# Attention scores from a relu, two linear columns per head and one VectorE operation per tile, with a fourth tile of receivers' rows expanded from windows

## The reference

```python
x_l = (x @ W_l + b_l).reshape(n, H, F)
x_r = (x @ W_r + b_r).reshape(n, H, F)
e_emb = (ea @ W_e).reshape(-1, H, F)
m = jax.nn.leaky_relu(x_l[src] + x_r[dst] + e_emb, 0.2)
alpha = jnp.einsum('ehf,hf->eh', m, att)
```

## Time and profile before

| | us |
|---|---|
| median of 3 runs | 6645.43 |
| lowest and highest | 6640.19, 6647.89 |
| span of the profiled execution | 5191.8 |
| TensorE busy in the span | 4139.6 (80%) |
| VectorE busy | 3632.4 (70%) |
| ScalarE busy | 2012.0 (39%) |
| GpSimd busy | 2560.2 (49%) |

### The profile page before, as it was taken

The page is one execution under the profiler, slowest core; times in us unless marked ns, Lnnn a source line. Parts: engine busy times, 40 slices in busy tenths (PEclk is TensorE's granted clock), DMA queues, the critical chain, the costliest instruction groups (busy, mean ns, idle before and its releaser), DMA issues. The chain is left out here.

```text
span 5191.8 us, 87147 instructions
## 1 busy us (share of the span) xinstructions
PE 4139.6 (80%) x27186; PEld 3591.2 (69%) x27186; DVE 3632.4 (70%) x9778; ACT 2012.0 (39%) x4938; POOL 2560.2 (49%) x2806
## 2 busy tenths in 40 slices
PE   5710677758888999999489999998788778887888
PEld 5610566757786666666377777788788778877888
DVE  8977578857776888888789999977344434444554
ACT  6835344434443333333244444456122212221222
POOL 0010777667774666666100000014777577757775
PEclk9955778778888999999789999975888888888888
DMA  8023677757774444444122222235566556655665
GB/s 216 7 40 78 154 186 187 181 122 156 160 158 107 105 105 105 104 104 104 31 63 53 53 54 52 51 90 141 124 135 136 116 123 136 135 120 120 135 135 114
DMA packets 1642255, 583.18 MB, mean 112 GB/s; under 512 B 1548519, under 2 KB 1574950, under 8 KB 1641578
## 3 DMA queue, kind: packets, MB, share of 16 engines
q1 hardware_dynamic: 921158, 297.65, 25.3%
q10 hardware_dynamic: 636612, 195.74, 16.2%
q0 software_dynamic: 84064, 84.64, 8.8%
HBM read 381.77 MB, written 209.21 MB: 114 GB/s over the span
## 5 line engine op out<-in xcount | busy, mean ns | idle before, releaser
L2002 POOL DMA_INDIRECT early<-node_g,src_w x1173 | 1114.6, 950 | 426.2 <-issue 356.5
L2219 POOL DMA_INDIRECT early<-node_g,src_w x782 | 759.4, 971 | 296.7 <-issue 248.8
L2784 POOL TENSOR_TENSOR fbt_c<-x_sb,fbln 128x128 f32<-128x128 f32 x56 | 22.3, 399 | 1026.2 <-DVE fbln L2860 1026.2
L1115 POOL DMA_INDIRECT fscat<-node_g,early x392 | 370.6, 946 | 287.7 <-PE bank L1147 136.6
L1221 ACT ACTIVATE fsy<-bank 128x512 f32<-128x512 f32 x448 | 243.8, 544 | 439.3 <-DVE fslz L1264 155.7
L2263 PE MATMUL bank<-l0S,l0msg 128*128 128x128 f32 x1568 | 277.8, 358 | 152.3 <-DVE l0S L2361 62.3
L2263 PEld LDWEIGHTS bank<-l0S,l0msg 128*128 128x128 f32 x1568 | 267.8, 270 | 159.5 <-issue 92.4
L2554 PE MATMUL bank<-early,faS 128*128 128x256 f32 x1568 | 357.8, 386 | 0.0
L1264 DVE TENSOR_TENSOR fslz<-bank,fsy 128x512 f32<-128x512 f32 x448 | 267.0, 621 | 117.6 <-ACT fsy L1221 105.7
L2554 PEld LDWEIGHTS bank<-early,faS 128*128 128x128 f32 x1568 | 296.5, 192 | 73.8 <-issue 34.9
L2044 PE MATMUL bank<-l3S,l3msg 128*128 128x128 f32 x1568 | 230.9, 316 | 104.0 <-issue 64.5
(11 more groups left out here) (363 smaller groups left out, 10924.8 us busy)
## 6 DMA issues: line engine op xcount, KB each, us to landing
edge_h<-early SPq DMA_DIRECT2D x280, 224.0 KB
node_g<-amax ACTq DMA_DIRECT2D x224, 224.0 KB
early<-edge_h SPq DMA_DIRECT2D x168, 256.0 KB
early<-node_g,src_w POOLq DMA_INDIRECT x1955
l0msg<-edge_a ACTq DMA_DIRECT2D x56, 256.0 KB
l0msg<-edge_h SPq DMA_DIRECT2D x56, 256.0 KB
l1msg<-edge_h SPq DMA_DIRECT2D x56, 256.0 KB
alpha<-edge_h SPq DMA_DIRECT2D x56, 256.0 KB
```

The source lines that it names most:

```text
L1115: pool.indirect_dma_start(out=cat[:, s, t, 0:F], out_offset=None, in_=node_g, in_offset=bass.IndirectOffsetOnAxis(ap=src_i[:, col], axis=0 ...
L2002: pool.indirect_dma_start(out=ring[:, n % RING, t, :], out_offset=None, in_=table_in, in_offset=bass.IndirectOffsetOnAxis(ap=src_w[:, n * ...
L2219: pool.indirect_dma_start(out=ring[:, n % RING, t, :], out_offset=None, in_=table_in, in_offset=bass.IndirectOffsetOnAxis(ap=src_w[:, n * ...
```

## The change

The leaky relu is written as 0.8 relu(z) + 0.2 z. The part 0.2 z times `att`, summed over a head, is linear in the inputs, so it becomes a column of the weights: each head gets two more columns, the sum of weight times `att` and its negative (`FX = 66`, `HX = 264`). relu of the one minus relu of the other gives the linear part back, with factors 0.2 and -0.2 in `att_x`. One operation of VectorE for each tile, max with 0 and then times `att_x`, makes what ScalarE's scaling, the max and the multiplication made; the sum over a head runs over 66 columns. A tile has a bank to itself, counted by `z_ok` and `z_read`.

The bias product uses 128 rows, of which all but three are zero, and two tiles' bias products stand together. `EXPAND` goes from 3 to 4. `turn_edges` makes all transposes first and then the products with `spread`. The node numbers that are compared are made once, for all steps, instead of in each. `own_rows(n)` moves between `turn_edges(n)` and `turn_own(n + 1)`. The widened weights are made at the start of the stage, and the bias rows in `attention_weights` get the two columns as well. Indents are cut in the diff, and the counts on which SP and ScalarE wait, which only change their names, are left out.

```diff
-EXPAND = 3
+EXPAND = 4
...
+FX = F + 2
+HX = HEADS * FX
...
-b3_row = sb("b3_row", [3, HF], bf16)
+b3_row = sb("b3_row", [P, HX], bf16)
...
-lz = tb("lz", [P, 2, HS, HF]); ones3 = tb("ones3", [3, P], bf16)
-y = tb("y", [P, 2, 2, HF])
+lz = tb("lz", [P, 2, HS, HX]); ones_b = tb("ones_b", [P, P], bf16)
+Wlr_x = tb("Wlr_x", [2 * F, HX]); Wea_x = tb("Wea_x", [F + 1, HX]); Wself_x = tb("Wself_x", [2 * F, HX])
+att_x = tb("att_x", [P, HX]); first_i = tb("first_i", [1, T], i32)
+by_head = lambda ap: ap.rearrange("p (h f) -> p h f", h=HEADS)
+weights = [(Wlr_x, Wlr, 2 * F), (Wea_x, Wea, F + 1), (Wself_x, Wself, 2 * F)]
...
-ids_ps = bank[3][:, HF:HF + EXPAND * SPAN].rearrange("p (w t) -> p t w", w=SPAN)
+assert NS * EXPAND * SPAN <= 512
+ids_ps = bank[3][:, 0:NS * EXPAND * SPAN].rearrange("p (w n t) -> p n t w", w=SPAN, n=NS)
...
-block_no = lambda n, kind, k: (2 * n + kind) * NB + k
-z_bank = lambda g: bank[4 + g % 4]
-att_ps = bank[3][:, 0:HF].unsqueeze(1).to_broadcast((P, HS, HF))
+tile_no = lambda n, kind, t: (2 * n + kind) * HS + t
+z_bank = lambda g: bank[4 + g % 4][:, 0:HX]
...
         if n >= 1:
             pe.wait_ge(catT_ok, n)
+        if n == 0:
+            pe.wait_ge(spread_ok, 1)
+        place = [(b, t, slice((t - t0) * P, (t - t0 + 1) * P)) for b, (t0, t1) in enumerate(CH) for t in range(t0, t1)]
+        for b, t, col in place[EXPAND:]:
+            nc.tensor.transpose(bank[b][:, col], cat[:, s, t, :], ident[:, :])
+        for b, t, col in place[:EXPAND]:
+            nc.tensor.transpose(bank[b][0:F, col], cat[:, s, t, 0:F], ident[:, :])
         pe.wait_ge(near_in[s], 16 * EXPAND * (n // 2 + 1))
         pe.wait_ge(spread_ok, n + 1)
-        for b, (t0, t1) in enumerate(CH):
-            for t in range(t0, t1):
-                col = slice((t - t0) * P, (t - t0 + 1) * P)
-                if t < EXPAND:
-                    nc.tensor.transpose(bank[b][0:F, col], cat[:, s, t, 0:F], ident[:, :])
-                    for w in range(SPAN):
-                        ins = nc.tensor.matmul(bank[b][F:2 * F, col], near[:, s, t, w, :], spread[:, t, w, :], start=(w == 0), stop=(w == SPAN - 1))
-                else:
-                    ins = nc.tensor.transpose(bank[b][:, col], cat[:, s, t, :], ident[:, :])
+        for b, t, col in place[:EXPAND]:
+            for w in range(SPAN):
+                ins = nc.tensor.matmul(bank[b][F:2 * F, col], near[:, s, t, w, :], spread[:, t, w, :], start=(w == 0), stop=(w == SPAN - 1))
         ins.then_inc(cat_turned, 1)
...
-        for k, (t0, t1) in enumerate(PAIRS):
-            g = block_no(n, OWN, k)
-            if g >= 4:
-                pe.wait_ge(lz_ok, g - 3)
+        for t0, t1 in PAIRS:
             for t in range(t0, t1):
-                to = z_bank(g)[:, (t - t0) * HF:(t - t0 + 1) * HF]
-                nc.tensor.matmul(to, ones3[:, :], b3_row[:, :], start=True, stop=False)
-                ins = nc.tensor.matmul(to, selfT[:, s, t * P:(t + 1) * P], Wself[:, :], start=False, stop=True)
-            ins.then_inc(z_ok, 1)
+                g = tile_no(n, OWN, t)
+                if g >= 4:
+                    pe.wait_ge(z_read, g - 3)
+                nc.tensor.matmul(z_bank(g), ones_b[:, :], b3_row[:, :], start=True, stop=False)
+            for t in range(t0, t1):
+                to = z_bank(tile_no(n, OWN, t))
+                nc.tensor.matmul(to, selfT[:, s, t * P:(t + 1) * P], Wself_x[:, :], start=False, stop=True).then_inc(z_ok, 1)
...
-        for k, (t0, t1) in enumerate(PAIRS):
-            g = block_no(n, EDGE, k)
-            pe.wait_ge(lz_ok, g - 3)
-            for t in range(t0, t1):
-                to = z_bank(g)[:, (t - t0) * HF:(t - t0 + 1) * HF]
-                nc.tensor.matmul(to, catT[:, t * P:(t + 1) * P], Wlr[:, :], start=True, stop=False)
-                ins = nc.tensor.matmul(to, eaT[:, s, t * P:(t + 1) * P], Wea[0:F + 1, :], start=False, stop=True)
-            ins.then_inc(z_ok, 1)
-
-    pe.wait_ge(padded, 1)
+        for t in range(HS):
+            g = tile_no(n, EDGE, t)
+            pe.wait_ge(z_read, g - 3)
+            nc.tensor.matmul(z_bank(g), catT[:, t * P:(t + 1) * P], Wlr_x[:, :], start=True, stop=False)
+            nc.tensor.matmul(z_bank(g), eaT[:, s, t * P:(t + 1) * P], Wea_x[:, :], start=False, stop=True).then_inc(z_ok, 1)
...
+    pe.wait_ge(first_ok, 1)
...
+    pe.wait_ge(padded, 1)
+    pe.wait_ge(w_copied, 1)
     turn_own(0)
     own_rows(0)
     for n in range(NS):
         turn_edges(n)
+        if n >= 1:
+            own_rows(n)
         if n + 1 < NS:
             turn_own(n + 1)
         edge_tiles(n)
-        if n + 1 < NS:
-            own_rows(n + 1)
...
-    def leaky(n, kind):
-        for k, (t0, t1) in enumerate(PAIRS):
-            g = block_no(n, kind, k)
-            act.wait_ge(z_ok, g + 1)
-            if g >= 2:
-                act.wait_ge(lz_ok, g - 1)
-            A.activation(y[:, g % 2, 0:t1 - t0, :], z_bank(g)[:, 0:(t1 - t0) * HF].rearrange("p (t c) -> p t c", c=HF), ACT.Copy, scale=SLOPE).then_inc(y_ok, 1)
-
+    for to, w, n_rows in weights:
+        ins = A.copy(by_head(to[:, :])[:, :, 0:F], by_head(w[0:n_rows, :]))
+    ins.then_inc(w_copied, 1)
     turned_own(0)
-    leaky(0, OWN)
     for n in range(NS):
         turned_edges(n)
         if n + 1 < NS:
             turned_own(n + 1)
-        leaky(n, EDGE)
-        if n + 1 < NS:
-            leaky(n + 1, OWN)
...
-    v.memset(ones3[:, :], 1.0)
+    v.tensor_scalar(first_f[:, :], dst_f[0:1, :], float(NP - SPAN * P), None, ALU.min)
+    v.tensor_scalar(first_i[:, :], dst_f[0:1, :], float(NP - SPAN * P), None, ALU.min)
+    v.drain()
...
+    v.memset(ones_b[:, :], 1.0)
...
+    v.tensor_scalar(by_head(att_x[:, :])[:, :, 0:F], by_head(attb[:, :]), 1.0 - SLOPE, None, ALU.mult)
+    v.memset(by_head(att_x[:, :])[:, :, F:F + 1], SLOPE)
+    v.memset(by_head(att_x[:, :])[:, :, F + 1:FX], -SLOPE)
+    product = [lz[:, 0, k, 0:HF] for k in range(len(weights))]
+    for to, (_, w, n_rows) in zip(product, weights):
+        v.tensor_tensor(to[0:n_rows, :], w[0:n_rows, :], attb[0:n_rows, :], ALU.mult)
+    v.drain()
+    for of, (to, _, n_rows) in zip(product, weights):
+        v.tensor_reduce(by_head(to[:, :])[:, :, F], by_head(of[0:n_rows, :]), AX.X, ALU.add)
+    v.drain()
+    for to, _, _ in weights:
+        v.tensor_scalar(by_head(to[:, :])[:, :, F + 1], by_head(to[:, :])[:, :, F], -1.0, None, ALU.mult)
...
+    by_step = first_id[:, 0:NS * HS].rearrange("p (n t) -> p n t", t=HS)[:, :, 0:EXPAND]
+    for w in range(SPAN):
+        v.tensor_scalar(ids_ps[:, :, :, w], by_step, float(w * P), None, ALU.add)
+    v.drain()
...
     def expand(n):
-        own = first_id[:, n * HS:n * HS + EXPAND]
-        for w in range(SPAN):
-            v.tensor_scalar(ids_ps[:, :, w], own, float(w * P), None, ALU.add)
         dve.wait_ge(dst_in[n % 2], 16 * (n // 2 + 1))
         if n >= 1:
             dve.wait_ge(cat_turned, n)
-        v.drain()
         v.tensor_tensor(spread[:, :, :, :], dst_b[:, n % 2, :].rearrange("p (t e) -> p t e", t=EXPAND).unsqueeze(2).to_broadcast((P, EXPAND, SPAN, P)),
-                        ids_ps.unsqueeze(3).to_broadcast((P, EXPAND, SPAN, P)), ALU.is_equal).then_inc(spread_ok, 1)
-        v.drain()
-
-    def leaky(n, kind):
-        for k, (t0, t1) in enumerate(PAIRS):
-            g = block_no(n, kind, k)
-            dve.wait_ge(y_ok, g + 1)
-            v.tensor_tensor(lz[:, kind, t0:t1, :], z_bank(g)[:, 0:(t1 - t0) * HF].rearrange("p (t c) -> p t c", c=HF), y[:, g % 2, 0:t1 - t0, :], ALU.max).then_inc(lz_ok, 1)
-        v.drain()
-
+                        ids_ps[:, n, :, :].unsqueeze(3).to_broadcast((P, EXPAND, SPAN, P)), ALU.is_equal).then_inc(spread_ok, 1)
 
     def scores(n, kind):
-        leaky(n, kind)
+        for t in range(HS):
+            g = tile_no(n, kind, t)
+            dve.wait_ge(z_ok, g + 1)
+            v.scalar_tensor_tensor(lz[:, kind, t, :], z_bank(g), 0.0, att_x[:, :], ALU.max, ALU.mult).then_inc(z_read, 1)
+        v.drain()
         to = (amax, alpha)[kind][:, n * HS:(n + 1) * HS, :]
-        v.tensor_tensor(lz[:, kind, :, :], lz[:, kind, :, :], att_ps, ALU.mult)
-        v.drain()
-        v.tensor_reduce(to, lz[:, kind, :, :].rearrange("p t (h f) -> p t h f", h=HEADS), AX.X, ALU.add).then_inc(scored, 1)
+        v.tensor_reduce(to, lz[:, kind, :, :].rearrange("p t (h f) -> p t h f", h=HEADS), AX.X, ALU.add)
 
     expand(0)
-    scores(0, OWN)
     for n in range(NS):
+        scores(n, OWN)
         if n + 1 < NS:
             expand(n + 1)
         scores(n, EDGE)
-        if n + 1 < NS:
-            scores(n + 1, OWN)
+    v.drain()
...
+    v.memset(b3_row[:, :], 0.0)
...
-    left = brb[0:3, :]
+    v.tensor_copy(brx[:, :, 0:F], brb[0:3, :].rearrange("p (h f) -> p h f", h=HEADS))
+    v.tensor_tensor(b_lin[0:3, :], brb[0:3, :], attb[0:3, :], ALU.mult)
+    v.drain()
+    v.tensor_reduce(brx[:, :, F], b_lin[0:3, :].rearrange("p (h f) -> p h f", h=HEADS), AX.X, ALU.add)
+    v.drain()
```

(56 more changed lines are left out.)

2 lines of the change are left out of this document (removed).

## The result

The kernel after took 6600.5 us (median of 7 runs, 6572.24 to 6628.33) against 6646.74 for the kernel before (7 runs): ratio 0.9924, 95% interval 0.9899 to 0.9949. The forecast was 6554, range 6507 to 6612.

The account below looks back on a forecast made before the run. TensorE was taken to bound `edge_rows`: 2.9 + 4.4 + 0.6 + 6.26 + 0.4 = 14.6 us a step against 16.17, 88 us, plus 4 once; span 5100 plus 1453.6 gives 6554 us, range 6507 to 6612.

Parts of the forecast that it names:

- TensorE bounds the stage, and the step shrinks by the pieces named: In `edge_rows`, TensorE sets the step, which goes from 16.17 to 14.6 us, 88 us over 56 steps.
- edge tiles with their wait: In `edge_tiles`, 14 products of 264 columns take 6.26 us, plus 0.4 waiting for VectorE.
- the switch cost of `own_rows`: TensorE going over to the bias product and back: 0.1 us per group, 0.4 for four groups.
- the wait for the copy: Before the edge products, TensorE's 0.62 us idle for ScalarE's copy to `catT` goes, covered by `own_rows` products.
- a wait in mid-edge: TensorE waits 0.4 us for VectorE before the fifth edge tile of each step.
- The price from the 448-wide row: VectorE's fused operation at 264 columns, priced from a 0.620 us operation on 448 elements: 0.43 us.
- Rival 2: VectorE becomes the bound: fused operation 0.69 us, step 15.4, gain 47 us, time 6598; chance 0.08.
- Rival 1: In `own_rows`, data type causes the switch: 0.3 us per group, step 15.4, time 6598; chance 0.18.
- Rival 3: TensorE's granted clock falls in `edge_rows`: at 0.86 the step is 16.9 us, time 6680; chance 0.07.
- Program size hardly changes, so I hold the time outside the span still: Whole launch: the median's 1453.6 us above the span stays, added to a span of 5100 us.
- The 92 us of gain: Whole kernel: 88 us from the 56 steps of `edge_rows` plus 4 us once per launch.
- Rival 4: No gain: `near` loads or GpSimd's restart arrive late by 1.6 us a step; time 6640, chance 0.05.

## Why the prediction was right or wrong

- *TensorE bounds the stage, and the step shrinks by the pieces named*: right on quick chips, where the stage is over at 2385 for the 2435 forecast. By pieces, forecast and measured (chip 13): edge tiles with their wait 6.66 and 6.67 (2003.60 to 2010.27), `turn_edges` 2.9 and 2.75 (to 2013.02), `own_rows` 4.4 and 3.92 (the rest of the step, to the transposes of `turn_own` one step on), `turn_own` 0.6 and 0.44. Together 14.6 and 13.78. The term most mis-sized is the switch cost of `own_rows`: I took 0.4 and it is 0.
- *Where the gain lies on a quick chip*: of the 2.39 us that a step loses, `own_rows` gives 1.86 (5.78 to 3.92) and the wait for the copy with `turn_own` 0.78 (1.22 to 0.44); `turn_edges` gives 0.15, and the edge tiles take 0.40 back. So TensorE itself gains by the bias product on 128 rows and by the move. The new form of the scores only costs it columns; what it brings is on VectorE, whose busy time in the stage falls from 779 to 621 us, from 13.9 a step to 11.1. With 13.9 VectorE alone would need more than the step of 13.78. The rewrite alone was not run, so its own share is not shown.
- *VectorE*: 0.43 an operation and a wait in mid-edge of 0.4. Measured are 0.43 and 0.41, as the edge tiles take 6.67 for 6.26 (the 0.56 in the row is the idle time of the weight loads). The price from the 448-wide row was exact. Rival 2 is out.
- *Rival 1, the switch is one of type*: out, by the run on 3 rows and by `own_rows` at 3.92, where it asked for 5.2.
- *Rival 3, the clock*: out for the quick chips, 0.99 in the stage. On chip 6 it stands at 0.94 before and 0.95 after, so it falls in both alike.
- *Program size hardly changes, so I hold the time outside the span still*: this step failed. There is next to no time outside the span. The 1453.6 us were the distance between two kinds of chips, most of it in other stages (`edge_rows` itself differs by some 110, 930 to 1039), and the sum was made for a chip on which the median had not been taken. The 92 us of gain were worked out from a quick trace and taken off a slow time. They are too few for a quick chip (145 measured) and too many for the slow ones (46, 34 and 8). That 6600.5 fell into the range is luck: it lies at the end that was put there for rivals 1 and 2, a gain of 34 to 47, and neither of them happened.
- *Rival 4, late loads and a late restart fill what TensorE gave up*: nearest to what the slow chips show. I gave it 0.05 because the slack in the trace was 2.5 and 5 us; in the slow traces the store goes out late enough to keep GpSimd idle for 6 us in the step shown. That this chain sets the time is not shown, and what starts the lateness is open.

## What to carry to other kernels

Set the span of the trace beside the median before building on either: a gap of a fifth is no overhead to be held constant but a sign that the trace and the times are of different conditions. Where a small product stands between full ones, give it all 128 rows, with zeros, rather than 3: it saved 0.29 us for each group here. A change worth 2.7% where one engine is the bound can be worth 0.1 to 0.8% where waits between queues are, so read slack against the slowest condition that the times show.

## What the runs showed of the hardware

The same program (the kernel before) took 5193 to 5198 us on two chips and 6551 to 6647 in three sets of runs of the slow kind. VectorE's operations keep their lengths (the fused one 0.426 us on chips 6 and 8, 0.431 on chip 13). But there are stretches of some us in which several engines together issue an instruction only every 0.7 us or not at all, and after some of them TensorE's products go at the pitch of 1.2 GHz. What starts these stretches stays open: halving the near packets did not change the time, one near load less, with a gather in its place, made it longer, and the DMA share in the stretch shown is 0.20, lower than before it.
